# First feed-forward with an order of its own for each engine: inputs prepared tiles ahead, block maxima in SBUF

## The reference

```python
x = x + 0.5 * _L0_ffn_ref(_layernorm(x), w_gate, w_up, w_down)
x = x + _L0_attn_ref(_layernorm(x), ...)
x = x + 0.5 * _L0_ffn_ref(_layernorm(x), w_gate, w_up, w_down)
x = x + 0.5 * _L1_ffn_ref(_layernorm(x), ...)      # ternary weights
x = x + _L1_attn_ref(_layernorm(x), ...)
x = x + 0.5 * _L1_ffn_ref(_layernorm(x), ...)

def fp4_quant_dequant(x):       # blocks of 16 along the last dimension
    scale = maximum(max(abs(xb), axis=-1) / 6.0, 1e-12)
    q = _GRID[searchsorted(_MID, abs(xb / scale))] * sign(xb) * scale

gate, y = fp4_linear(x, w_gate), fp4_linear(x, w_up)    # 256 -> 704 each
h = silu(gate) * y
return fp4_linear(h, w_down)                            # 704 -> 256
```

## Time and profile before

| | |
|---|---|
| median of three runs | 2732.37 us (2726.93 to 2732.46) |
| the profiled execution | 2731.94 us, span 2730.0 us, mean granted clock 0.979 |
| busy: TensorE matmul / weight load | 92% / 79% of the span |
| busy: VectorE / ScalarE / GpSimd | 68% / 51% / 47% |
| DMA | 45.97 MB, mean 17 GB/s |
| first matmul of the stage's tile loop to the next stage's first, S = 0 | 37.40 to 573.61 us |
| the same for S = 2 | 1005.30 to 1535.65 us |

### The profile page before, as it was taken

The page is one execution under the profiler, slowest core; times in us unless marked ns, Lnnn a source line. Parts: engine busy times, 40 slices in busy tenths (PEclk is TensorE's granted clock), DMA queues, the critical chain, the costliest instruction groups (busy, mean ns, idle before and its releaser), DMA issues.

```text
span 2730.0 us, 77893 instructions
## 1 busy us (share of the span) xinstructions
PE 2521.5 (92%) x32232; PEld 2164.1 (79%) x32232; DVE 1847.3 (68%) x4324; ACT 1405.8 (51%) x2345; POOL 1271.7 (47%) x1382
## 2 busy tenths in 40 slices
PE   4999999989999989989999899999999999979999
PEld 3777778878888877777778788887888888858888
DVE  7887777756767778888876466645665566645664
ACT  3554445433333435444444588865444444418886
POOL 5777777731111127777777423211443344462221
PEclk8999999989999999999999899999999999979999
DMA  5000000000100110000000000000000000000001
GB/s 177 1 6 1 1 1 1 1 12 22 24 21 23 24 49 1 1 1 1 1 1 1 17 1 1 1 9 19 17 17 17 17 17 18 17 6 24 32 32 39
DMA packets 67566, 45.97 MB, mean 17 GB/s; under 512 B 13184, under 2 KB 66192, under 8 KB 67216
## 3 DMA queue, kind: packets, MB, share of 16 engines
q1 hardware_dynamic: 67216, 41.00, 5.4%
HBM read 15.78 MB, written 8.40 MB: 9 GB/s over the span
## 4 chain that ended last, share of the span: by engine, by line
PE 39%; POOL 27%; issue 21%; DVE 6%; ACT 5%; DMA 0%; POOLq 0%; SPq 0%; DVEq 0%; ACTq 0%
POOL fHTL L767 6%; PE ps L1433 4%; PE ps L46 4%; POOL fV L754 4%; POOL fHX L761 4%; PE ps L1434 4%; PE ps L48 4%; PE ps L47 4%; PE ps L1450 3%; PE ps L1448 3%; PE ps L1070 2%; PE ps L982 2%; PE ps L258 2%; POOL fXV L349 2%; DVE XTL L268 2%
## 5 line engine op out<-in xcount | busy, mean ns | idle before, releaser
L1500 DVE TENSOR_TENSOR gHl<-gHf,gHh 128x512 fp32r<-128x512 f32 x256 | 191.0, 746 | 208.0 <-ACT gHh L1477 207.6
L46 PE MATMUL ps<-WGH,XTH 128*128 128x512 f32 (+1 forms) x768 | 313.8, 409 | 10.1 <-ACT fSG L670 6.7
L227 POOL TENSOR_SCALAR ve<-mv 128x4 f32<-128x4 f32 x96 | 22.9, 238 | 627.4 <-DVE mv L219 623.4
L767 POOL TENSOR_TENSOR fHTL<-fHTF,fHTH 128x768 fp32r<-128x768 f32 x128 | 236.0, 1844 | 169.1 <-ACT fHTF L665 169.1
L48 PE MATMUL ps<-WGL,XTH 128*128 128x512 f32 (+1 forms) x768 | 291.0, 379 | 0.0
L47 PE MATMUL ps<-WGH,XTL 128*128 128x512 f32 (+1 forms) x768 | 289.2, 377 | 0.0
L46 PE MATMUL ps<-WDH,fHTH 128*128 128x256 f32 (+1 forms) x768 | 239.4, 312 | 24.5 <-issue 22.4
L245 ACT ACTIVATE XN<-X,nb,rs 128x256 f32<-128x256 f32 x384 | 206.9, 589 | 104.5 <-POOL nb L233 104.5
L1448 PE MATMUL ps<-W2T,gHh 128*128 128x256 f32 x1024 | 255.6, 283 | 0.0
L1450 PE MATMUL ps<-W2T,gHl 128*128 128x256 f32 x1024 | 253.0, 281 | 0.0
L1433 PE MATMUL ps<-XTH,W1T 128*128 128x512 f32 x512 | 205.6, 402 | 21.4 <-DVE XTL L268 18.8
(11 more groups left out here) (237 smaller groups left out, 7096.4 us busy)
## 6 DMA issues: line engine op xcount, KB each, us to landing
X<-in_x SPq DMA_DIRECT2D x16, 512.0 KB, 8.8
a0vp<-a0vt SPq DMA_DIRECT2D x256, 32.0 KB, 2.3
a1vp<-a1vk SPq DMA_DIRECT2D x256, 32.0 KB, 2.2
out<-X SPq DMA_DIRECT2D x16, 512.0 KB, 2.9
tws<-in_w SPq DMA_DIRECT2D x2, 1024.0 KB, 7.7
WN<-in_wgu SPq DMA_DIRECT2D x3, 384.0 KB, 6.9
a0km<-in_wqkv SPq DMA_DIRECT2D x2, 384.0 KB, 3.3
a1pry<-in_aw SPq DMA_DIRECT2D x1, 768.0 KB, 4.5
```

What stands on the lines that cost most here:

```text
L46: e.matmul(o, hh, mh, start=first, stop=False)
L767: pool.tensor_tensor(HTL[(n - 3) % 2][:, :, :], HTF[:, :, :], HTH[(n - 3) % 2][:, :, :].bitcast(F32), ALU.subtract).then_inc(s_hlo, 1)
L1500: dve.tensor_tensor(Hl[m % 8][:, :], Hf[m % 4][:, :], Hh[m % 8][:, :].bitcast(F32), ALU.subtract).then_inc(s_hl, 1)
```

## The change

All engines' order in the loop of the first feed-forward is written anew:

- TensorE: up(0,0) ahead of the loop; then in step n up(n,1), turn(n-3), up(n,2), up(n+1,0), the input transposes at j = 1 and 2, out(n-4).
- ScalarE: silu of tile n comes first, then the evictions of tile n-3, the magnitude of tile n-1, and after them input work, with the norms in two halves (rows 2 and 3 of a chunk at j = 0, rows 0 and 1 of the next chunk at j = 3).
- VectorE: input work for the tile, then H to reciprocal of tile n (`hidden`), both steps of tile n-1 together, set-up work, and the X add of tile n-4 last.
- GpSimd: fHTL of tile n-3, fV of tile n, fHX of tile n-1, then input work at j = 0, 1 and 2.
- Statistics run three to four chunks ahead; `x_max` is a function of its own, one tile ahead of `x_scale`. The first two chunks of the next stage are in the same stream.
- Block maxima (of tiles, inputs and weights) go to the SBUF tiles `rc` and `xrc` in place of PSUM, and both tensor_scalars are awaited before the reciprocal. The wait of the maxima on the magnitude is gone; waits on the statistics' and norms' buffers come in, as they are now reused across engines further apart.
- The set-up steps move from n = 34, 38 and 22 to 33, 37 and 21.

```diff
 # stats and spread
                 if k == 4:
                     dve.wait_ge(s_bn, F + 1)
+                    if F > 1:
+                        dve.wait_ge(s_nb, 2 * F - 3)
...
             pool.wait_ge(s_ag, F + 1)
+            if F > 1:
+                pool.wait_ge(s_xn, F - 1)
...
-        am = PS[5][:, 256:300]
...
+        def x_max(dve, S, i):
+            g = 8 * S + i
+            dve.wait_ge(s_xn, 16 * S + i + 1)
+            if g:
+                dve.wait_ge(s_qxv, g)
+            dve.tensor_reduce(xrc[:, :], s3(xf), AX, ALU.max, apply_absolute_value=True).then_inc(s_qxam, 1)
...
 # ffn0_pe
+            up(0, 0)
             for n in range(NT):
                 i, j = n // 4, n % 4
-                if n >= 5:
-                    out(n - 5)
+                up(n, 1)
+                if n >= 3:
+                    turn(n - 3)
+                up(n, 2)
+                if n + 1 < NT:
+                    if j == 3:
+                        pe.wait_ge(s_xl, 2 * (16 * S + i + 1) + 2)
+                    up(n + 1, 0)
...
+                if j in (1, 2):
+                    x_turn_pe(pe, S, i + 1, j - 1)
+                if n >= 4:
+                    out(n - 4)
+            for n in range(NT - 3, NT):
+                turn(n)
+                out(n - 1)
+            out(NT - 1)
...
 # ffn0_act, at the head of step n
+                if n < NT:
+                    act.wait_ge(s_gu, 3 * t + 2)
                     if n > 1:
-                        act.wait_ge(s_hq2, q)
-                    act.activation(mag.bitcast(R32), V[(n - 1) % 2][:, :], ACT.Abs, scale=MAGIC).then_inc(s_ha, 1)
+                        act.wait_ge(s_hm, t - 1)
+                    act.activation(SG[n % 2][:, :], PSA[:, 0:NF], ACT.Silu).then_inc(s_sg, 1)
...
 # ffn0_act, at its end
+                    if j == 0 and i + 1 < NS:
+                        x_mag(act, S, i + 1, 1)
+                    if n == 0:
+                        norm(act, S, 2, (0, 1))
+                    if j == 0 and i + 2 <= NS:
+                        norm(act, *chunk(16 * S + i + 2), (2, 3))
+                    if j in (1, 2):
+                        x_turn_act(act, S, i + 1, j - 1)
+                    if j == 3 and i + 2 < NS:
                         x_mag(act, S, i + 2, 0)
+                    if j == 3 and i + 3 <= NS:
+                        norm(act, *chunk(16 * S + i + 3), (0, 1))
...
 # ffn0_dve
+            for n in range(NT + 4):
                 t = tb + n
+                if 0 < n < NT:
+                    inputs(n)
+                if n < NT:
+                    hidden(n)
+                if n == 0:
+                    inputs(n)
+                if 1 <= n < NT + 1:
+                    v = V[(n - 1) % 2][:, :]
+                    dve.wait_ge(s_ha, t)
                     step_up(dve, v, mag).then_inc(s_hq1, 1)
+                    dve.wait_ge(s_hq1, t)
                     step_down(dve, v, mag).then_inc(s_hq2, 1)
...
+                if n >= 4:
+                    dve.wait_ge(s_dn, t - 3)
+                    dve.scalar_tensor_tensor(out=X[:, n - 4, :], in0=down, scalar=0.5,
+                                             in1=X[:, n - 4, :], op0=ALU.mult, op1=ALU.add).then_inc(s_xd, 1)
```

The new VectorE functions that this loop calls. `inputs(n)` does, by j: 0, x_grid of the first half and bn_aggr of chunk i+3; 1, x_grid of the second half and x_max; 2, x_low of the first half and x_scale; 3, x_low of the second half and bn_stats of chunk i+4. At n = 0 it also does all the statistics of chunk 2 and those of chunk 3. And:

```diff
+            def hidden(n):
+                t, u = tb + n, n % 2
+                dve.wait_ge(s_sg, t + 1)
+                dve.wait_ge(s_gu, 3 * t + 3)
+                if n > 1:
+                    dve.wait_ge(s_hv, t - 1)
+                dve.tensor_tensor(H[u][:, :], PSA[:, NF:NG], SG[u][:, :], ALU.mult).then_inc(s_hm, 1)
+                dve.wait_ge(s_hm, t + 1)
+                dve.tensor_reduce(rc[u][:, :], s3(H[u][:, :]), AX, ALU.max, apply_absolute_value=True).then_inc(s_ham, 1)
+                dve.wait_ge(s_ham, t + 1)
+                dve.tensor_scalar(sn[:, :], rc[u][:, :], 1.0 / 6.0 / NUDGE, 1e-12 / NUDGE, ALU.mult, ALU.max)
+                if n > 2:
+                    dve.wait_ge(s_hx, t - 2)
+                dve.tensor_scalar(sc[n % 3][:, :], rc[u][:, :], 1.0 / 6.0, 1e-12, ALU.mult, ALU.max).then_inc(s_hsn, 1)
+                dve.wait_ge(s_hsn, t + 1)
+                dve.reciprocal(rc[u][:, :], sn[:, :]).then_inc(s_hrc, 1)
```

More of the change, by code:

```diff
@@ L241, in norm @@
                     act.wait_ge(s_qxv, 8 * S + i)
+                elif S in (1, 3) and i == 0:
+                    act.wait_ge(s_qxv, 8 * (S - 1) + NS)
                 elif F:
@@ L333, in x_mag @@
             act.wait_ge(s_qxv, g + 1)
+            if h == 0 and i:
+                act.wait_ge(s_xl, 2 * (16 * S + i))
             if h:
@@ L371, in before_dve @@
             dve.memset(PSA[64:128, 3712:3840], 0.0).then_inc(s_hz, 1)
+            x_max(dve, 2, 1)
             x_scale(dve, 2, 1)
-        def before_act(act):
-            x_mag(act, 2, 1, 0)
         def before_pool(pool):
@@ L429, in start_dve @@
             grid(0)
+            x_max(dve, 0, 0)
             x_scale(dve, 0, 0)
@@ L451, in start_dve @@
             low(5)
+            x_max(dve, 0, 1)
             x_scale(dve, 0, 1)
@@ L687, in ffn0_dve, with inputs @@
             tb = 32 * S
-            for n in range(NT + 5):
-                t = tb + n
-                u = n % 2
-                i, j = n // 4, n % 4
-                if 2 <= n < NT + 2:
-                    q = t - 2
-                    v = V[n % 2][:, :]
-                    dve.wait_ge(s_ha, q + 1)
-                    step_up(dve, v, mag).then_inc(s_hq1, 1)
-                if n >= 5:
-                    dve.wait_ge(s_dn, t - 4)
-                    dve.scalar_tensor_tensor(out=X[:, n - 5, :], in0=down, scalar=0.5,
-                                             in1=X[:, n - 5, :], op0=ALU.mult, op1=ALU.add).then_inc(s_xd, 1)
-                if 2 <= n < NT + 2:
-                    dve.wait_ge(s_hq1, q + 1)
+            def inputs(n):
+                i, j = n // 4, n % 4
+                if j < 2 and i + 1 < NS:
+                    x_grid(dve, S, i + 1, j)
+                if n == 0:
+                    for k in range(8):
+                        stats(dve, S, 2, k)
+                    for k in range(4):
+                        stats(dve, S, 3, k)
+                if j == 0 and i + 3 <= NS + 1:
+                    for k in range(4, 8):
+                        stats(dve, *chunk(16 * S + i + 3), k)
+                if j == 1 and i + 2 < NS:
+                    x_max(dve, S, i + 2)
+                if j > 1:
+                    x_low(dve, S, i + 1, j - 2)
+                if j == 2 and i + 2 < NS:
+                    x_scale(dve, S, i + 2)
+                if j == 3 and i + 4 <= NS + 1:
+                    for k in range(4):
+                        stats(dve, *chunk(16 * S + i + 4), k)
@@ L1221, in attn0_dve @@
                 if n == NT - 4:
-                    dve.wait_ge(s_sc, 4 * (NT - 5) + 4)
+                    x_max(dve, 2, 0)
                     x_scale(dve, 2, 0)
@@ L1267, in ffn1_set_sp @@
                              src.rearrange("(k p) n -> p k n", p=P)).then_inc(d_w[n], 16)
-        when1 = (*range(8, 16), 17, 22, *range(24, 32), 33)
+        when1 = (*range(8, 16), 17, 21, *range(24, 32), 33)
         def ffn1_set_dve(dve, step):
```

147 lines of the change are left out of this document (41 added, 106 removed).

## The result

Before 2732.41 us, after **2712.36 us** (medians of four runs each; after from 2711.26 to 2716.82): 0.9934 of the time before, 95% interval 0.9917 to 0.9952. The change wins 20 us. Forecast were 65, and the time lies above the range's high end of 2708.

What follows compares the result with a forecast made beforehand. TensorE sets the pace but also waits: 31.5 us a round against 28.8 without waits. Runs -38.4 and -25.6, fills -3.7 and -0.9, last tiles -0.8 sum to -69.4; +4 for jitter gives -65, 2667 us, range 2645 to 2708.

Steps and rivals of the forecast that it cites:

- The 1.20 us for fXV: TensorE's idle ahead of a round's first input transpose, waiting for GpSimd; 1.20 us a round, claimed to go.
- the 0.65 at `out`: TensorE's wait in one tile of a round for ScalarE's late fHTF eviction; 0.65 us, claimed to go.
- both 0.37: Waits in two tiles of a round, fHX transposes behind the X add that frees their PSUM bank; 0.37 us each, to go.
- VectorE's walk: One tile through VectorE's new order: X add ends 0.5 us before the transposes need it; load 25.7 of 28.8 us a round.
- Ternary rounds: Second run, tiles 24 to 31: VectorE also makes ternary weights and bounds at 34.5 us a round; 11.4 us stay.
- the wait at tile 21: Second run: TensorE waits for ternary scales standing behind `hidden` and both steps on VectorE; 3 us.
- Rival 4: Better than the sum: no jitter, ternary rounds spread load into neighbours' slack; 2655 us, chance 0.66 together with the forecast.
- jitter: Small slacks met over 28 rounds: 0.15 us a round taken off the gain, +4 us.
- First fill: First run's first tiles, up to the start of `up(4,1)`: from 73.35 to 69.6, -3.7 us.
- Drain: From `up(63,1)` to the next stage's first matmul: same TensorE order, -1 to +1, taken as 0.
- Rival 1: The wait only moves: hand-overs 0.5 to 0.7 us longer make transposes or `out` wait in every tile; about 2702 us, chance 0.22.
- Rival 2: VectorE bound, slower than before: reduce into SBUF and x_max run at 3.4 ns an element beside GpSimd; about 2808, chance 0.08.

Runs made afterwards that it cites:

- e12: Changed kernel with the tiles' maxima in SBUF as 11 rows of 4, one element apart, read there by both tensor_scalars; no wait added: 2679.2 us.
- e3: Changed kernel with VectorE's set-up work behind the X add instead of ahead of it, except at n=21: 11 us less.
- e2: Kernel before, in its old order, with only the tiles' maxima moved to SBUF: +45 us.
- e9: e7 with the 16 ternary-weight operations behind tiles 1 and 2 of a round instead of 0 and 2: 1.4 us a round less.
- e10: e6 with set-up work behind the X add, ternary operations placed as in e9, other set-up steps spread over tiles 1 and 2 too: 2669.4 us.
- e13: e12 with e10's order of the set-up work: 2670.9 us.
- e6: Changed kernel with maxima read from SBUF, but the first tensor_scalar writes to PSUM, where the reciprocal and second tensor_scalar read: 2678 us.
- e7: e4 (e1 and e3 together, 2687.6 us) with the 16 ternary-weight operations one by one behind every second tile: eight rounds of 31.1 us.
- e8: e7 with the norm of chunk 2 behind silu(1) and its maxima behind tile 1's steps: nothing won.
- e11: Changed kernel, both tensor_scalars of a tile naming their destination as 11 touching rows of 4; the wait is unchanged, no total time given.
- e1: Changed kernel with the tiles' maxima back in PSUM, written by the reduce and read by both tensor_scalars there: 2695 us.
- e5: Changed kernel with the first tensor_scalar of a tile writing every second column, and the second one likewise in every third tile: 2705.8 us.

## Why the prediction was wrong

**What bounds the kernel: right.** A better order lets TensorE run through. The floor of 28.8 us a round, worked out from starts in the earlier trace rows, is 28.96 in e12, with no idle at all in the round. The 1.20 us for fXV, the 0.65 at `out` and, once the tensor_scalar is short, both 0.37 went.

**VectorE's walk: the step that failed.** The prediction gave the waits for both tensor_scalars "some 0.1 us each", with the cost of block maxima in SBUF inside the 0.2 us a tile that it added to VectorE's load, and it put what GpSimd could add at 2 or 3 us for the whole kernel. It was 0.52 us on average and up to 1.3 for the first tensor_scalar alone, an operation of 44 elements. The walk had 0.5 us of slack from the X add to the transposes; this ate it in most tiles. Price: 1041.4 - 1012.7 = 29 us for the two runs (after against e12), of the 45 that are missing there (forecast 1065.7 - 69.4 = 996.3).

The rows for it stood in the prediction. Line 1304, two SBUF inputs, at 1760 ns: I read a slower rate, 3.4 ns an element, and feared it for the reduce. It was 0.75 us of work and a wait until fHX ended, as e3 showed. In the changed kernel both sides of it can be seen:

```profile
1226.17 0.48 DVE L1325 TENSOR_SCALAR ta<-tws,ta 128x512 f32<-128x512 f32 x1
1226.34 1.56 POOL L789 TENSOR_TENSOR fHX<-fV,fsc 128x704 f32<-128x704 f32 x1 [0.28 <-DVE fV L305]
1226.69 1.75 DVE L1327 SCALAR_TENSOR_TENSOR W2T<-tws,ta 128x512 fp32r<-128x512 f32 x1
...
1227.98 0.55 POOL L231 TENSOR_SCALAR ve<-mv 128x4 f32<-128x4 f32 x1
1228.37 0.41 DVE L765 SCALAR_TENSOR_TENSOR X<-ps,X 128x256 f32<-128x256 f32 x1
...
1228.88 0.85 PE L604 MATMUL ps<-ident,fHX 128*128 128x128 f32 x6 [2.05 <-POOL fHX L789]
```

Line 1325 starts first and takes its 0.48; fHX, begun beside it, takes 1.56 in place of 1.39. Line 1327 comes while fHX runs and ends 0.54 us behind it; GpSimd's next operation, on 4 elements, takes 0.55 in place of 0.23. Whoever is first goes on, the other stands still, and the profile counts the standing as busy. The question to ask was not "at what rate does it run beside GpSimd" but "for how long does GpSimd have the memory when it comes": GpSimd is busy 24 of 30 us a round, in pieces of 1.4 to 1.9 us.

The prediction's sentence on the Trainium skill used a page that is right and says too little: GPSIMD Engine Reference (Specifications) says that there is contention. The Trainium skill's SBUF — State Buffer ("SBUF: two separate sides") says how: the port pair is "an exclusive lock, not a bandwidth split", and whichever "starts first gets the pair for the whole instruction; the other fully blocks". It names VectorE's operations in a two-port mode and those with two SBUF inputs. The rows of fHTL, x_scaled, fHX and line 1327 agree, and in e12 an operation that the mode doesn't fit has no wait. Line 229 in e2 doesn't agree: the tensor_scalar ran through beside it in 28 tiles of 28. By the Trainium skill's rule the price is what GpSimd still has to do when the tensor_scalar comes: 0.93 and 1.04 us in the two tiles shown.

**Ternary rounds: two nearly right, one wrong.** Forecast were 34.5 us for a round of ternary tiles, from VectorE's load of 25.7 + 8.8, and 3 us for the wait at tile 21. Counted from one x_scaled to the next, tile 21 and the eight ternary tiles lie in three rounds, the first with tile 21 and one ternary tile: by the forecast 33.2, 34.5 and 33.1 us. The changed kernel has 37.0, 38.0 and 36.3; without the tensor_scalar's wait (e12) they are 37.6, 35.9 and 33.7. So with the wait gone the second and third are 1.4 and 0.6 us above the forecast, and the first 4.4. Load isn't what makes that one long:

```profile
1124.07:1161.63 37.56, 32.81 (x182) 28.43 (x181) 27.83 (x59) 16.04 (x25) 24.07 (x19) 0.91 0.00 1
```

VectorE is busy in 27.8 of its 37.6 us. TensorE's wait at tile 21 is 3.06 us, as large as forecast; what the forecast put at nothing, without saying so, is the granted clock of 0.91 in this round, at which TensorE is busy for 32.8 us in place of 29.0. Over the 14 rounds of the second run the changed kernel's clock is 0.98 (before: 1.00), and TensorE's busy time rose from 410.5 to 414.3 us.

Rival 4's clause, that these rounds could spread their load into their neighbours, is what e9, e10 and e13 show: second run 425.0 to 412.0 us (e12 to e13), of which 4 are in the round with tile 21, at 0.95 in place of 0.91.

**What is left of the gap.** The two runs of e13 take 1001.2 us against the forecast's 996.3, but that doesn't close the account: the forecast's sum has 11.4 us for the crowded rounds that e13 avoids. The fair comparison is e12, which has the set-up work where the changed kernel has it: 1012.7, 16 us over. 9 of them are in the rounds (412.1 against 408.2 us, 425.0 against 419.9), the others ahead of and behind these 14 rounds. The 4 us that the forecast allowed for jitter can cover a part.

**Small terms.** First fill (the first tiles, in which the engines still wait for their first inputs): 35.95 to 32.65 us from the first `up` to `up(4,1)`, -3.3 for a forecast -3.7; second 28.96 to 28.87, -0.1 for -0.9. First run's set-up rounds were taken at 1 us for VectorE; in e12 they cost 5 (31.2, 30.8 and 30.0 us against 29.0). Drain (the last tiles), from `up(63,1)` to the next stage: 31.5 to 33.1 and 33.0 to 33.8 us, +1.6 and +0.8 where I had 0. Outside the two runs 3.6 us were added. The last 1195 us, in which all kernels are alike, range from 1193.3 to 1201.2 in the fifteen profiles, and they go along with the granted clock: in the three shortest (e6, e7, e8) it is at its lower level for 39 to 40 us of this stretch, in the longest (e11) for 58. Why it is there for longer in one execution than in another stays open.

**Rivals.** Rival 1 (2702) comes nearest in time and by its sign, transposes 0.1 us behind the X add. But its mechanism, hand-overs longer than taken, isn't there: e12 has the same order and no wait. Rival 2 had the right engine and the wrong operation; the reduce kept its 0.89 us. That the kernel is still faster is due to the order: the memory move by itself costs 45 us (e2), the order with the tiles' maxima left in PSUM wins 37 (e1), and with the maxima in SBUF and no wait 53 (e12).

## What to carry to other kernels

Before an operand moves from PSUM to SBUF, look at what GpSimd is doing at that moment: a VectorE tensor_scalar with both ends in SBUF may stand still until a large GpSimd operation ends, however few its own elements, and the profile shows that as a long operation, not as idle. A mean duration that differs between like operations, or from the same operation elsewhere, wants its minimum, median and maximum and the neighbour's end beside it. And work put into an engine's slack is free only where nothing behind it in the queue is awaited: the same two operations cost 2.0 us a round behind tiles 0 and 2, and 0.6 behind tiles 1 and 2.

## What the runs showed of the hardware

- A tensor_scalar of 44 fp32 elements, SBUF to SBUF: 0.19 us with GpSimd idle; with GpSimd's fHTL under way 0.50 to 1.54 in 117 tiles of 118, ending 0.04 to 0.05 us behind it. Beside GpSimd's power on 4 elements (line 229 in e2) it takes 0.19 in 28 tiles of 28. A stride of two on the destination (e5), or rows that touch (e11), don't change the wait; a source in rows one element apart gives 0.20 in all 128 tiles (e12), a PSUM source 0.20 (e1), a PSUM destination 0.21 (e6).
- A reduce from SBUF to SBUF doesn't wait: line 730 takes 0.89 us at 464.27 too, where GpSimd's fHTL runs from 464.23 to 466.08.
- A scalar_tensor_tensor with two SBUF inputs, 512 elements: 0.75 us alone, 1.75 to 2.31 beside GpSimd's operations, which are held up in turn (0.23 to 0.55 us, 1.39 to 1.56, 1.94 to 2.38).
- The granted clock of TensorE falls from 1.00 to the lower level during a wait of 3.06 us (e10, e13, tile 21). A round's matmuls are busy for 33.44 us at a mean of 0.86, 30.44 at 0.95 and 28.96 at 1.00 (e12).
